# An attention and expert kernel: the value products move between the scores of two heads and those of the other two

## What is computed

```python
# x: (2048, 128); layer 1: 16 heads of 8, causal, then layernorm and Wo
qk = einsum('bthd,bshd->bhts', qh, kh);  attn = softmax(where(causal, qk, -inf))
o1 = layernorm(einsum('bsdh,bhts->bthd', vh, attn)) @ Wo.T
# layer 2: rmsnorm, rope, 16 query heads on 4 key heads, causal attention
x = x + (attend(q, k, v) * sigmoid(gate)) @ Wo;  h2 = rmsnorm(x)
e = argmax(h2 @ Wr)                    # one of 8 experts per token
y = expert_e(h2)                       # W1, gate, W2
```

## Time and profile before

| | |
|---|---|
| median of 3 runs | 962.51 us |
| profiled execution, time / span | 962.84 / 960.8 us |
| TensorE busy | 830.7 us (86%) |
| ScalarE busy | 602.9 us (63%) |
| VectorE busy | 552.4 us (57%) |
| GpSimd busy | 227.1 us (24%) |
| mean granted TensorE clock | 0.945 |

### The profile page before, as it was taken

How to read it: one execution, slowest core, us unless ns; L and a number is a source line. 1 busy time by engine, 2 the same in 40 slices (tenths; PEclk the granted TensorE clock), 3 DMA queues, 4 the chain that set the end, 5 groups by cost and what they waited for, 6 DMA issues and landing times.

```text
span 960.8 us, 16941 instructions
## 1 busy us (share of the span) xinstructions
PE 830.7 (86%) x5303; PEld 306.4 (32%) x5384; DVE 552.4 (57%) x1095; ACT 602.9 (63%) x771; POOL 227.1 (24%) x438
## 2 busy tenths in 40 slices
PE   4711979999988999999899999999999999978991
PEld 2311223333322333333223332232333334314650
DVE  7884436666634666665256665664899726514524
ACT  2433847777767776777767777777555676655331
POOL 7392131201120112011201120124011212171533
PEclk9765889999999999999999999999999999989995
DMA  3425440030032001101310021023000030112003
GB/s 67 143 87 194 126 81 1 2 99 2 14 98 93 1 1 38 64 1 51 97 57 1 2 66 35 1 76 103 24 1 1 5 131 2 47 45 61 31 23 99
DMA packets 39398, 49.74 MB, mean 52 GB/s; under 512 B 10476, under 2 KB 29712, under 8 KB 39304
## 3 DMA queue, kind: packets, MB, share of 16 engines
q1 hardware_dynamic: 38056, 45.99, 16.0%
q0 software_dynamic: 1248, 2.57, 0.8%
HBM read 36.82 MB, written 11.42 MB: 50 GB/s over the span
## 4 chain that ended last, share of the span: by engine, by line
PE 70%; DVE 9%; issue 6%; ACT 6%; SPq 5%; DMA 2%; POOL 1%; ACTq 0%; DVEq 0%; POOLq 0%
PE PS L1051 25%; PE PS L1036 21%; PE PS L1014 12%; ACT PR L890 5%; DVE MP L1364 3%; PE PS L1190 3%; PE PS L1067 2%; SPq L563 2%; SPq L557 2%; PE PS L1210 1%; PE PS L1018 1%; DVE CROW L1301 1%; DMA q_parts<-QA 1%; PE PS L1189 1%; PE PS L974 1%
## 5 line engine op out<-in xcount | busy, mean ns | idle before, releaser
L890 ACT ACTIVATE PR<-PS 128x1024 f32<-128x1024 f32 (+3 forms) x640 | 539.5, 894 | 239.2 <-PE PS L1036 237.2
L1364 DVE TENSOR_REDUCE MP<-PS 128x1 f32<-128x512 f32 (+3 forms) x640 | 367.1, 607 | 209.9 <-PE PS L1014 115.7
L1036 PE MATMUL PS<-QA,KA 128*128 128x512 bf16 (+3 forms) x1199 | 321.9, 352 | 47.4 <-DMA QA<-CROW 20.4
L1051 PE MATMUL PS<-PR,VA 128*32 128x512 f32 (+3 forms) x2560 | 306.1, 551 | 13.1 <-POOL PR L782 10.9
L782 POOL TENSOR_SCALAR_AFFINE_SELECT PR<-PR 128x256 f32<-128x256 f32 x256 | 102.4, 409 | 515.7 <-ACT PR L890 513.0
L1014 PE MATMUL PS<-MB 72*128 72x512 bf16 (+3 forms) x640 | 216.2, 352 | 5.9 <-DVE MP L1364 4.3
L1036 PEld LDWEIGHTS PS<-QA,KA 128*128 128x128 bf16 x1280 | 99.7, 98 | 249.4 <-ACT PR L890 164.1
L1014 PEld LDWEIGHTS PS<-MB 72*128 72x128 bf16 x640 | 60.2, 97 | 131.5 <-DVE MP L1364 87.1
L1051 PEld LDWEIGHTS PS<-PR,VA 128*32 128x32 f32 x2560 | 51.0, 108 | 114.0 <-issue 84.8
L1018 PE MATMUL PS<-CM,IDB 128*128 128x128 bf16 x256 | 54.9, 221 | 0.0
L1383 DVE COPY OT<-PS 128x512 f32<-128x512 f32 x32 | 21.9, 685 | 53.0 <-PE PS L1051 52.9
(11 more groups left out here) (206 smaller groups left out, 466.9 us busy)
## 6 DMA issues: line engine op xcount, KB each, us to landing
QA<-q_parts SPq DMA_DIRECT2D x96, 96.0 KB
KA<-k_parts SPq DMA_DIRECT2D x96, 96.0 KB
MB<-q_parts SPq DMA_DIRECT2D x48, 96.0 KB
MB<-k_parts SPq DMA_DIRECT2D x48, 96.0 KB
q_parts<-QA SPq DMA_DIRECT2D x8, 384.0 KB, 2.5
k_parts<-QA SPq DMA_DIRECT2D x8, 384.0 KB, 2.7
MB<-in_L_ffn_W SPq DMA_DIRECT2D x1, 2048.0 KB, 8.6
expert_tokens<-ZERO SPq DMA_DIRECT2D x1, 1483.5 KB, 10.0
```

The source lines that it names most:

```text
L890: act.activation(PR[:, tile % RING, :, 0:CH - q0], PS[:, 2 * p:2 * p + 2, 0:CH - q0], ACT.Exp).then_inc(s_ex, 1)
L1036: last = pe.matmul(PS[:, 2 * p + k, 0:CH - q0], KA[:, b, kb // BPC, 2 * p + k, kb % BPC * P:(kb % BPC + 1) * P], QA[:, b, c, 2 * p + k, q0 ...
L1051: last = pe.matmul(PS[32 * hh:32 * hh + 32, 6, q0:CH], VA[:, b, kb, hh, :], PR[:, (2 * s + hh // 2) % RING, hh % 2, 0:CH - q0], start=kb = ...
L1364: dve.reduce_max(MP[:, BPC * (HG * (qb // BPC) + hh) + qb % BPC, kc:kc + 1], PS[:, unit_bank(u, peeled), 0:w], AX).then_inc(s_mr, 1)
```

## The change

In every step, `values` is issued behind the first half's scores and part 0 of the maxima, ahead of the second half's scores and part 1. Nothing is added or removed, and no other engine's order changes. VectorE's, ScalarE's and GpSimd's programs are as before.

```diff
--- before.py
+++ after.py
@@ -1077,14 +1077,14 @@
                 if s == BPC:
                     pe.wait_ge(s_lk[side % 2], 16 * NLATE * (i + 1 + side // 2))
                 parts = units_at(maxima_of(peeled, side), s) if side < 2 else ((), (), ())
+                side_v, v = behind(side, s, LAG)
                 for p in range(2):
                     if s < NS:
                         scores(i, side, s, p)
                     for item, hh in parts[p]:
                         max_unit(i, item, hh, peeled)
-                side_v, v = behind(side, s, LAG)
-                if v < NS and side_v >= 0:
-                    values(i, side_v, v)
+                    if p == 0 and v < NS and side_v >= 0:
+                        values(i, side_v, v)
                 side_t, t = behind(side, s, LAG + 1)
                 if ending(t) is not None and side_t >= 0:
                     turn(i, side_t, ending(t), peeled)
```

## The result

The changed kernel took 988.39 us in the median of 4 runs (985.69 to 995.98), beside 962.31 us before (median of 4 runs, too): 1.0283 times as long (95% interval 1.0223 to 1.0343), 26 us slower. The forecast was 979 us, 966 to 989: the right sign and not enough. The profiled execution is the slowest of the four, 995.98 us; its mean granted clock was 0.932, that of the others 0.946 to 0.951.

The account below looks back on a forecast made before the run. TensorE's own queue order was taken to bound nearly all steps. Terms 8.4 + 5 + 5 + 1.5 - 1.7 gave +18 us; from the median, rounded down a little, 979 us, range 966 to 989.

Parts of the forecast that it names:

- term 5: Values waiting for masks or the chunk's copy in four places: second scores and part 1 behind them come late, +1.5 us.
- Term 2: Pair loop: bunched maxima wait for banks, 5.5 us a turn, 2.7 of old waits go; net +8.4 us, bounds +2 to +16.
- Term 3: Last pair's side 0, three banks: bursts of maxima wait for banks, some 13.5 us against 8.4 now; net +5, bounds 0 to +10.
- Term 4: 31 transposes and 20 feed-forward pieces, now behind a bf16 product, each pay 0.10 us to enter: +5 us, lower bound zero.
- Term 6: Steps without maxima: values fill waits for exponentials, -2.5 us, and the loop's turns cost +0.8; net -1.7 us.
- term 4 at nothing: Rival "entry free": entering transposes and feed-forward products costs nothing, 974 us, 30%.
- the one of VectorE: Rival: VectorE bound in last pair, old waits kept in loop, terms 2 and 3 at upper bounds, +16 and +10: 992 us, 15%.

Follow-up runs that it names:

- the copy out of the way: Changed kernel with one VectorE edit, the copy of a finished chunk ahead of part 1 of the maxima: 1.0183 times the kernel before.
- bunching alone: Kernel before with part 1 of the maxima moved behind the value products, and the chunk's copy ahead of part 1 on VectorE: 1.0188 times before.
- halved reductions: Changed kernel with every maximum taken over half of its columns: 973.7 us, 1.0109 times the kernel before.
- the two runs that switch it: Kernel before with the change only in the last pair's side 1: 1.0060; changed kernel with the old order there: 1.0226 times before.
- the second trace of before: Kernel before, unchanged, profiled once more for its trace; steps with maxima repeat to 0.02 us.
- the old order in the last side: Changed kernel with the old order in the last pair's side 1: 984.0 us, 1.0226 times before.
- the combination: Kernel before with maxima spread round values in loop sides 1 and last side 0, the change in the last side's first 16 steps: 964.68 us, 1.0013.

## Why the prediction missed

The forecast added 18 us, of which 979 us keeps 16.5; measured are 26 us, about 27 by the ratio. The step that failed is in term 5: it took the waits in front of value products to be the four that were there already, and put nothing for a new one. The runs showed 16 waits for the chunk's copy in its place, worth 7.7 us in the loop.

- **Term 2, bunched maxima in the loop: right.** Forecast +8.4 us net; with the copy out of the way 8.3 us were measured. The waits stand where they were placed, 0.3 us behind a three-unit step of 512-wide units. In the experiment with bunching alone it was 11 us; the 2.7 us between the two experiments I did not take apart.
- **Term 3, the last pair's side 0: right in kind, a little small.** +5 forecast, +6.7 measured, bunching alone +6.8. With halved reductions the stretch from step 3 to 33 fell below its length of before, so the time is VectorE's release of banks. VectorE's own busy time there didn't grow (85.5 us for 88.0), but that didn't bring the lower bound of 0.
- **Term 4, transposes and feed-forward products enter alone: wrong, and of the wrong sign.** Forecast 51 x 0.10 = +5 us. A transpose behind a bf16 maximum starts 0.22 us after it and takes 0.43 to 0.44, against 0.49 behind values, so 31 transposes save some 1.5 us. Feed-forward pieces start 0.44 us behind two 512-wide scores, the scores' own time, and most are shorter, too: four transposes take 0.44 us for 0.49, two products of 512 columns 0.86 for 0.96. In the last side's first 16 steps that makes some 0.9 us. I had taken the price from a row whose bf16 product uses 24 rows of the array. The rule of the Trainium skill (TensorEngine Tiling (Array Packing), section Key Properties), that a change of tiling mode drains the array, would put the 0.1 us at the strips of values, and the trace agrees with that: entering values still costs it (0.31 us behind a maximum), entering a transpose of full size doesn't.
- **Term 5, waits in front of values: the step that failed.** It counted four places where values wait already and priced the scores behind them. It left out that the move makes a new wait. VectorE's order is part 1, then copy; part 1 was issued ahead of the values and is now issued behind them and behind the second scores, so the copy starts 1.8 us behind the start of its chunk's last values and not 0.7, and the next chunk's values need the bank. 16 waits, 8.5 us, one of them (1.8 us) in the last side; undoing it gave 7.7 us back in the loop. The prediction even used the copy in step 29 of side 1, as a delay of a maximum, and did not ask who else waits for it.
- **Term 5 again, the last side: too small.** The masks' waits were priced at 0.2 us each, for the scores behind them. But their release is set by GpSimd, so what TensorE gains earlier turns into wait; ScalarE runs dry; and behind the longer wait TensorE's clock is granted at half for some time. Forecast +0.8 for places in the last side, measured +6.1 from step 16 to 39 and up to 7 more in the expert stage of the profiled execution. That the order of this side costs some us is shown by the two runs that switch it; how the us divide between wait, clock and chance is read from single traces, and stays open.
- **Term 6, ScalarE's feed: right in sign, the size not settled.** -1.7 forecast; the exit of the loop gained 1.2 and the last side's start 1.8 us, but about half of the latter is the 0.9 us of term 4. Waits for exponentials went from 15.6 to 12.0 us, as forecast, but were 13.1 in the second trace of before and 15.0 in that of the changed kernel. The turns can't be read to better than some us.

The sum by terms as measured is 8.3 + 7.7 + 6.7 - 0.6 - 1.8 + 6.1 + 6.9 = 33 us for the profiled execution's 33.1 (the transposes' gain is inside the first three); the others, with a higher clock, are 6 to 10 us below it. Of the median's 26 us the first three, which repeat, are 22.8; terms 2 and 3 had 13.4 of them.

Two of the forecast's sums are off by little: with term 4 at nothing they give 975.7 us, not 974, and their upper ends 993.3, not 992. Of the rivals, the one of VectorE (992 us) had the time nearly right by luck. Its +16 us in the loop are the measured 16.1, but half of them is the copy: with that out of the way 8.3 were left.

## What to carry to other kernels

When work is moved in one engine's queue, go through the other engines' queues as well: each keeps its order, so whatever stands there behind an operation that is now fed later is late too, and its own waiters with it. With two buffers, look at which producers become neighbours, not only at what is between them on average: here 2.3 units a step were no problem and three in a row were. And a wait whose release is set by another engine swallows any gain in front of it, while everything moved behind it is late by its full length.

## What the runs showed of the hardware

The same program repeats a loop side of 79 us to 0.02 us in two profiles, while stretches with a wait of 3 us or more for another engine differ by up to 4 us between executions (30.4 and 34.5 us for one turn of the loop). The granted clock has a part in it: after the wait of 3.81 us it was 0.54 of full, and the two steps behind took 2.62 us each for 1.33 and 1.75 in the repeated trace of before, where the wait was 1.87 us and the clock stayed at 1.00 (866 to 872 us). The wait was dearer than its length, here by some 2 us. What decides whether the clock falls stays open. At that place, in the 6 us from the waiting values' start, it was 0.72 after waits of 1.83 us (first profile of before), 3.10 and 3.13 us (the old order in the last side; the combination), and the two steps took 4.6 to 4.7 us together each time; it was 0.56 to 0.59 after the four waits of 3.8 to 4.0 us. The Trainium skill, TensorE: Matmul & The Clock Gate, Part 1, describes the gate with its two levels, 1.2 and 2.4 GHz.
